# Feed-forward through 32 moment and position features per 128-long segment instead of all 512 inputs, weights built once, and one state chunk in eight weighed on VectorE

## The chip, the cores and the metric

One of the eight cores of a Trainium2 chip runs the whole program in one launch. The metric is the device time of one execution in microseconds (us). TensorE (PE; its weight loads are PEld), VectorE (DVE), ScalarE (ACT), GpSimd (POOL) and SyncE (SP) run side by side and meet only at semaphores.

## What is computed

Two layers over x (4 batches x 512 positions x 512 features). The change lies in the second and third lines:

```
x += attention of layer 0 (keys and queries from ctx), on layernorm(x)
x += down_w @ (silu(gate_w @ h) * (up_w @ h)),   h = layernorm(x)        # 2048 inner rows
x += selective scan (512 channels, 16 states, 512 steps) from ctx, gated by silu(layernorm(x))
x += mixture of experts (32 experts, 8 per token), on layernorm(x)

spline weights:   w[n] = cubic in f between control points,  n = 0 .. 2048*512-1
                  t = linspace(0, NCTRL-1, n);  i = floor(t);  f = t - i      # NCTRL = n / 128.9
scan, per state:  state = state * exp(dt * A) + (dt * u) * B[t];   y += state * C[t]
```

A control point covers 128.9 consecutive weights. So any 128 consecutive weights of a row lie on at most two cubics, that of control interval i and the next, and where the second takes over is known beforehand (the masks).

## The kernel before, in words

Four blocks follow each other: `block_a` (attention, inputs of the scan, and 24 cubic coefficients per 512 weights, `coef_d`), `block_b` (scan and feed-forward), `block_c` (gating, router) and `block_d` (experts). The change is in `block_a` and above all in `block_b`.

`block_b` interleaves two jobs that share no data. The **scan** takes 64 steps `s` (4 batches x 16 states); a step works on four chunks of 128 channels x 512 positions. For each step POOL multiplies the input by the row B (`drive`, L1156) into the tile `E`, ACT makes the decay (`decay`, L889) into one of two banks `dA`, DVE runs the recurrence (`scan`, L1024), POOL multiplies three chunks by the row C (`weigh`, L1162), DVE the fourth, whose state lies in a bank (`weigh_last`, L1030), and a DMA of POOL's queue adds 1 MB of products to `y_d` in HBM (`gather`, L1173). POOL's own order is `weigh(s)`, `drive(s + 2)`, `gather(s)`. `E` has four buffers (`drive(s + 2)` waits until the transfer of step s - 2 has landed), the rows B and C have three between them (`BC`, loaded by SP), `dA` two (`decay` m waits for `scan` m - 2). Each of these chains is in the order written out by hand.

The **feed-forward** takes 32 turns `jj`, two steps each: turn `jj` does 256 inner rows (group `jj // 4`) for one batch (`jj % 4`). The weights of a group are built from coefficients by 6 units (`weights`, `unit_first`, `blend`, `unit_lo`): PE evaluates the two cubics of 128 x 512 weights (L781, L784), DVE picks by mask (L991, L995), ACT and DVE split the result in a high and a low part (L867, L1000). The eight groups take 48 units. A turn's `gate_up` is 2 chunks x 2 matrices x 4 K-slices x 3 products (high*high, high*low, low*high; L794 to L796), 48 matmuls of type fp32r. Then come `silu` (ACT, L879, between two loads of ACT's function table: exp, silu, exp), `mult` (DVE, L1006), `down` (4 tiles x 2 matmuls in full fp32, L806) and four `add`s to x (DVE, L1011). The last `mult` and `down` stand behind the last statistics of x (`late_sums`, L1016).

The two products with the row C before:

```python
            def weigh(s):
                ...
                g.tensor_tensor(E[:, s % NR, 0:NW, :], E[:, s % NR, 0:NW, :], spread(BC[op % NBC][:, :], NW), ALU.mult).then_inc(prod_done, 1)
            def weigh_last(s):
                ...
                v.tensor_tensor(E[:, s % NR, NW, :], dA[(KC * s + NW) % 2][:, :], BC[op % NBC][:, :], ALU.mult).then_inc(last_done, 1)
```

## Time and profile before

| | us |
|---|---|
| median of 3 runs | 1568.68 (1562.31 to 1570.82) |
| span of the profiled execution | 1567.3 |
| up to the end of `block_a` | about 180 |
| `block_b` | about 180 to 818 |
| first `weigh` to the last `weigh` of the 64 steps | 198.66 to 798.60 |
| `block_c` and `block_d` | 818 to 1567.3 |

The profiled execution's time beyond its span is not recorded; its span lies 1.4 us under the median. Busy time over the whole span: PE 1435.0, DVE 1153.4, POOL 1062.3, ACT 918.4. A busy PE is not a PE at its peak, since matmuls overlap in its pipeline; the distance between the starts of two matmuls says more. In the rows below, idle time stands in square brackets with what ended it.

### The profile page before, as it was taken

How to read it: one execution, taken by the hardware profiler on the slowest of the kernel's cores; microseconds unless marked ns; L12 is line 12 of the kernel's file. 1: busy time of each engine (PE TensorE's matmuls, PEld its weight loads, DVE VectorE, ACT ScalarE, POOL GpSimd, SP SyncE). 2: the span in 40 equal slices, each digit the busy share in tenths (PEclk: the TensorE clock that was granted, in tenths of full speed). 3: DMA queues.
4: the chain of work that ended last, by engine and by line, in shares of the span. 5: the costliest groups of instructions: out<-in, count | busy, mean ns of one | idle time of the engine just before them, and what ended most of it. 6: DMA issues, size and time to landing. Idle time of an engine off the chain costs nothing. (4 is left out here: it accounts for less than half of the span.)

```text
span 1567.3 us, 26498 instructions
## 1 busy us (share of the span) xinstructions
PE 1435.0 (92%) x6453; PEld 1073.9 (69%) x6454; DVE 1153.4 (74%) x2069; ACT 918.4 (59%) x1420; POOL 1062.3 (68%) x654
## 2 busy tenths in 40 slices
PE   6999878999999999999975559989999999999997
PEld 3444556666666666666644238878988888898886
DVE  5888897888888878888878786656666666565554
ACT  6777677666667666766646664444544444444442
POOL 2222287999999989999941235757666676666675
PEclk9999989999999999999988759999999999999999
DMA  8232557888899889988869416889998899888876
GB/s 314 96 111 98 180 132 144 179 197 205 192 196 217 186 195 178 221 188 195 176 150 336 159 31 159 193 193 209 198 200 192 191 206 201 203 186 190 189 146 118
DMA packets 106416, 283.95 MB, mean 181 GB/s; under 512 B 16641, under 2 KB 18850, under 8 KB 95090
## 3 DMA queue, kind: packets, MB, share of 16 engines
q0 software_dynamic: 43520, 155.57, 50.0%
q1 hardware_dynamic: 60322, 123.12, 26.4%
q10 hardware_dynamic: 2512, 4.52, 0.8%
q8 instruction: 27, 0.44, 0.1%
q14 instruction: 35, 0.29, 0.1%
HBM read 152.28 MB, written 135.08 MB: 183 GB/s over the span
## 5 line engine op out<-in xcount | busy, mean ns | idle before, releaser
L1156 POOL TENSOR_TENSOR B_E<-B_dtu,B_BC 128x512 f32<-128x512 f32 (+3 forms) x121 | 309.3, 2670 | 16.7 <-DMA B_BC<-bc_d 16.7
L2080 POOL DMA_INDIRECT out_x<-D_y,D_rows x144 | 243.8, 1693 | 75.4 <-issue 43.6
L889 ACT ACTIVATE bank<-B_dtv,negA 128x512 f32<-128x512 f32 x256 | 173.5, 690 | 159.8 <-DVE B_E L1024 98.1
L1024 DVE TENSOR_TENSOR_SCAN B_E<-bank,B_E 128x512 f32<-128x512 f32 x192 | 230.2, 1214 | 42.5 <-ACT bank L889 34.8
L1162 POOL TENSOR_TENSOR B_E<-B_E,B_BC 128x1536 f32<-128x1536 f32 x64 | 234.0, 3656 | 34.5 <-DVE B_E L1024 29.8
L2045 POOL DMA_INDIRECT D_rows<-rows_d,D_source x144 | 155.9, 1083 | 129.0 <-DMA out_x<-D_y,D_rows 62.3
L806 PE MATMUL bank<-B_Wd,B_inter 128*128 128x512 f32 x512 | 231.9, 606 | 9.0 <-DVE X L1011 5.3
L1906 ACT ACTIVATE D_xT_hi<-bank 128x512 fp32r<-128x512 f32 x147 | 88.1, 599 | 231.5 <-PE bank L1815 167.8
L1826 PE MATMUL bank<-W_gu_hi,D_xT_hi 128*128 x584 | 202.4, 347 | 14.5 <-ACT D_xT_hi L1906 13.9
L1968 DVE TENSOR_TENSOR D_xT_lo<-bank,D_xT_hi 128x512 fp32r<-128x512 f32 x147 | 101.3, 689 | 141.1 <-ACT D_xT_hi L1906 108.7
L1827 PE MATMUL bank<-W_gu_lo,D_xT_hi 128*128 x584 | 199.2, 341 | 0.0
L806 PEld LDWEIGHTS bank<-B_Wd,B_inter 128*128 128x128 f32 x512 | 98.3, 195 | 122.8 <-issue 102.8
L1832 PE MATMUL bank<-W_gu_hi,D_xT_lo 128*128 x584 | 131.8, 348 | 6.8 <-DVE D_xT_lo L1968 5.5
L1946 ACT ACTIVATE D_y<-bank 128x512 f32<-128x512 f32 x144 | 86.4, 600 | 83.2 <-PE bank L1899 63.6
L1826 PEld LDWEIGHTS bank<-W_gu_hi,D_xT_hi 128*128 128x128 f32 x584 | 111.1, 190 | 27.5 <-issue 22.2
L1832 PEld LDWEIGHTS bank<-W_gu_hi,D_xT_lo 128*128 128x128 f32 x584 | 103.3, 191 | 18.6 <-DVE D_xT_lo L1968 14.0
L1827 PEld LDWEIGHTS bank<-W_gu_lo,D_xT_hi 128*128 128x128 f32 x584 | 111.2, 190 | 5.5
L794 PE MATMUL bank<-hT_hi,B_Wg_hi 128*128 128x512 f32 x256 | 105.4, 412 | 7.3 <-DVE hT_lo L1064 7.3
L2032 DVE TENSOR_TENSOR W_gu_lo<-W_raw_gu,W_gu_hi x30 | 52.8, 1761 | 66.4 <-ACT W_gu_hi L1916 51.3
L795 PE MATMUL bank<-hT_lo,B_Wg_hi 128*128 128x512 f32 x256 | 100.8, 394 | 0.0
L796 PE MATMUL bank<-hT_hi,B_Wg_lo 128*128 128x512 f32 x256 | 100.3, 392 | 0.0
L1011 DVE TENSOR_TENSOR X<-bank,X 128x512 f32<-128x512 f32 x128 | 86.7, 678 | 18.2 <-PE bank L806 18.2
(327 smaller groups left out, 3263.7 us busy)
## 6 DMA issues: line engine op xcount, KB each, us to landing
y_d<-B_E POOLq DMA_DIRECT2D x64, 1024.0 KB, 10.7
B_BC<-bc_d SPq DMA_DIRECT2D x128, 256.0 KB, 6.2
W_raw_gu<-in_wgu SPq DMA_DIRECT2D x64, 384.0 KB
W_raw_d<-in_wd SPq DMA_DIRECT2D x64, 256.0 KB
X<-in_x SPq DMA_DIRECT2D x4, 1024.0 KB, 9.2
y_d<-A_du SPq DMA_DIRECT2D x4, 1024.0 KB, 4.0
dt_d<-A_dtv SPq DMA_DIRECT2D x4, 1024.0 KB, 3.9
dtu_d<-A_dtu SPq DMA_DIRECT2D x4, 1024.0 KB, 4.1
```

Of the source, the lines that this page charges most:

```text
L794: pe.matmul(ps[:, :], hi, h_hi, start=k == 0, stop=False)
L806: mm = pe.matmul(Yb[t % 2][:, :], chunk(jj, ch)[:, t * P:(t + 1) * P], Wd[w][:, ch, :], start=ch == 0, stop=ch == 1)
L889: act.activation(dA[m % 2][:, :], dtv[:, c, :], ACT.Exp, scale=negA[:, c, n:n + 1]).then_inc(dA_done, 1)
L1024: v.tensor_tensor_scan(state, dA[m % 2][:, :], E[:, s % NR, c, :], 0.0, ALU.mult, ALU.add).then_inc(s_done, 1)
L1156: g.tensor_tensor(E[:, s % NR, c:end, :], dtu[:, at:at + end - c, :], spread(BC[op % NBC][:, :], end - c), ALU.mult).then_inc(dbu_done, 1)
L1162: g.tensor_tensor(E[:, s % NR, 0:NW, :], E[:, s % NR, 0:NW, :], spread(BC[op % NBC][:, :], NW), ALU.mult).then_inc(prod_done, 1)
L1826: pe.matmul(ps, *operands(k, xT_hi, W.gu_hi), start=k == 0, stop=False)
L1827: pe.matmul(ps, *operands(k, xT_hi, W.gu_lo), start=False, stop=False)
L1832: mm = pe.matmul(ps, *operands(k, xT_lo, W.gu_hi), start=False, stop=k == KC - 1)
L1968: v.tensor_tensor(xT_lo[i % 2][:, :], pT[:, :], xT_hi[i % 2][:, :], ALU.subtract).then_inc(xT_sb, 1)
L2045: g.indirect_dma_start(rows[i], None, rows_d[:, :], bass.IndirectOffsetOnAxis(ap=source[i // HALF][:, i % HALF:i % HALF + 1].bitcast(U32), ...
L2080: g.indirect_dma_start(a["out"], bass.IndirectOffsetOnAxis(ap=rows[i][:, ROW - 1:ROW].bitcast(U32), axis=0), ysb[:, i, :], None, compute_o ...
```

## The change

The feed-forward's weights of 128 consecutive inputs are a cubic in the position within the segment, so a product with h needs only the sums of h * position^p (p = 0..3). Instead of multiplying by 512 inputs, each turn first makes 4 x 32 features of h (`features`: for each segment of 128 inputs, the four moments of up to two runs of positions that share one side of every mask, and the few positions left over as they are), and multiplies these 128 features by weights `V` on features. For the runs to be few, the inner rows are sorted by where their second cubic begins, in groups of 256.

Per turn, `gate_up` is then 2 chunks x 2 matrices x 3 products on one K-slice, 12 matmuls; `features` is 4 full-fp32 matmuls with 32 columns of weights each, at four column positions of the array, whose result ACT copies (`feature_hi`) and DVE splits (`feature_lo`). The weights of all groups fit on chip, so they are built once: 24 units in turns 0 to 6 (8 for gate and up with 32 coefficients, 16 for down with 64 rows), in full fp32, with masks and powers loaded four units ahead through ACT's queue. The turns go batch by batch (`jj // 8` is the batch); h is transposed for one batch at a time, at three batch boundaries. `down` sums four chunks of 128 inner rows in one bank (two tiles of x a turn, 4 matmuls each), so there are two `add`s a turn. `silu` runs twice in a row. The last two turns' `down`s come ahead of the last statistics, except for their last two tiles.

In the scan, POOL's `weigh` takes three chunks in even steps and two in odd ones; DVE multiplies the third chunk there, ahead of `weigh_last`. In `block_a` DVE no longer splits the coefficients (12 instructions), the powers are no longer copied by ACT, and the table is loaded in four parts.

```diff
-NSEL = 3 * 2 * KC * 4
+NSEL = 2 * KC * 4
+NCH = INTER // P
+NF = P // KC
+TURN_UNITS = [[("gate_up", 1)] + [("down", k) for k in range(3)]]
+TURN_UNITS += [[("gate_up", g)] + [("down", 3 * (g - 1) + k) for k in range(3)] for g in (2, 3, 4)]
+TURN_UNITS += [[("gate_up", 5)] + [("down", k) for k in range(12, NCH)], [("gate_up", 6)], [("gate_up", 7)]]
+UNITS = [("gate_up", 0)] + [u for units in TURN_UNITS for u in units]
+NAHEAD = 4
...
+            later = second[:, own * KC + c]
+            edges = [0] + [e for e in range(1, P) if (later[e] != later[e - 1]).any()] + [P]
+            runs = sorted(zip(edges[:-1], edges[1:]), key=lambda run: run[0] - run[1])[:2]
+            alone = [e for e in range(P) if not any(lo <= e < hi for lo, hi in runs)]
+            assert 4 * len(runs) + len(alone) <= NF
+            for k, (lo, hi) in enumerate(runs):
+                for p in range(4):
+                    f = 4 * k + p
+                    summed[lo:hi, g, c, f] = power[p, lo:hi]
+                    for ab in range(2):
+                        to[ab, c, p, ab, c * NF + f] = 1.0
+                    masks[g, c * NF + f] = np.tile(later[lo], 2)
+            for k, e in enumerate(alone):
+                f = 4 * len(runs) + k
+                summed[e, g, c, f] = 1.0
+                for ab in range(2):
+                    to[ab, c, :, ab, c * NF + f] = power[:, e]
+                masks[g, c * NF + f] = np.tile(later[e], 2)
...
-                for n in range(3):
-                    v.wait_ge(c_hi, b * 3 + n + 1)
-                    v.tensor_tensor(coef[LOW, n, :], bank[2 + n][LOW, :], coef[LOW, n, :], ALU.subtract).then_inc(c_lo, 1)
...
+        NI, NBC, NR, NDU = 8, 3, 4, KC + 1
+        inter = sb("inter", [P, NI, L])
...
+        def sums_at(jj):
+            return [4 * (jj // 2 - 1) + 2 * (jj % 2) + i for i in range(2)] if jj >= 2 else []
+        def sum_tile(n):
+            return n // 16 * LT + n % 4
+        def pool_chunks(s):
+            return NW - s % 2
...
+            def weights(m):
+                n = unit_job(m)
+                kind, u = UNITS[m]
+                if m >= NAHEAD:
+                    pe.wait_ge(ld_unit[m % NAHEAD], 32 * (m // NAHEAD))
+                if kind == "gate_up" and u:
+                    pe.wait_ge(ld_coef, 16 * (u + 1))
+                if kind == "down" and u == 0:
+                    pe.wait_ge(ld_down, 16 * 2 * NCH // KC)
                 pair_free(n)
...
                 for ab, ps, done in ((0, first_bank(n), a_ps), (1, second_bank(n), b_ps)):
...
+                    if kind == "gate_up":
+                        pe.matmul(ps[:, :], powers[0:NSEL, m % NAHEAD, ab, :], coef[:, :], start=True, stop=True).then_inc(done, 1)
                     else:
-                        mm = pe.matmul(ps[:, :], powers[:, 2 * (g % 2) + unit - 4, ab, :], (coef[:, :] if g else first_down), start=True, stop=True)
-                    mm.then_inc(done, 1)
+                        pe.matmul(ps[:, :], powers[:, m % NAHEAD, 0, :], down_coef[:, ab, :], start=True, stop=True).then_inc(done, 1)
+            def features(jj):
+                g = jj % NG
+                if jj == 0:
+                    pe.wait_ge(ld_coef, 16)
+                if jj:
+                    pe.wait_ge(f_lo, jj)
+                if g == 0:
+                    pe.wait_ge(hT_done, LT * (jj // NG + 1))
+                for c in range(KC):
+                    mm = pe.matmul(F_bank[c * NF:(c + 1) * NF, :], summed[:, g, c, :], hT[:, c, :], start=True, stop=True, tile_position=(0, c * NF))
+                mm.then_inc(f_ps, 1)
             def gate_up(jj, ch):
-                n, w, tb = chunk_job[(jj, ch)], jj // 4 % 2, jj % 4
+                n, g = chunk_job(jj, ch), jj % NG
+                pe.wait_ge(f_lo, jj + 1)
+                if jj < NG:
+                    pe.wait_ge(used, unit_job(unit_of("gate_up", g)) + 1)
                 pair_free(n)
...
+                for ps, col, done in ((first_bank(n), ch * P, a_ps), (second_bank(n), GW + ch * P, b_ps)):
+                    hi, lo = (V[:, g, col:col + P] for V in (V_hi, V_lo))
+                    pe.matmul(ps[:, :], hi, F_hi[:, :], start=True, stop=False)
+                    pe.matmul(ps[:, :], hi, F_lo[:, :], start=False, stop=False)
+                    pe.matmul(ps[:, :], lo, F_hi[:, :], start=False, stop=True).then_inc(done, 1)
+            def down(n, ps):
+                quarter, t = n // 4, n % 4
+                if n < 16:
+                    pe.wait_ge(used, unit_job(unit_of("down", 4 * quarter + 3)) + 1)
+                pe.wait_ge(used, chunk_job(2 * quarter + 1, 1) + 1)
+                if quarter == NB * 4 - 1:
+                    if t >= 2:
+                        pe.wait_ge(add_done, n - 1)
+                elif n:
+                    pe.wait_ge(add_done, n)
+                if t == 0 and quarter == NB * 4 - 1:
+                    pe.wait_ge(add_done, n)
+                for i in range(4):
+                    mm = pe.matmul(ps[:, :], chunk(4 * quarter + i)[:, t * P:(t + 1) * P], Wd[:, (4 * quarter + i) % NCH, :], start=i == 0, stop=i == 3)
+                mm.then_inc(y_ps, 1)
             def turn(t):
                 pe.wait_ge(xn_done, t + 1)
-                if t >= 2:
+                if t % LT >= 2:
                     pe.wait_ge(hT_done, t - 1)
+                elif t >= LT and t % 2 == 0:
+                    pe.wait_ge(f_lo, NG * (t // LT))
+                elif t >= LT:
+                    pe.wait_ge(add_done, sums_at(NG * (t // LT) - 2)[-1] + 1)
                 for k in range(KC):
-                    mm = pe.transpose(Yb[t % 2][:, k * P:(k + 1) * P], xn[t % 2][:, k * P:(k + 1) * P], ident[:, :])
+                    mm = pe.transpose(T_bank[t % 2][:, k * P:(k + 1) * P], xn[t % 2][:, k * P:(k + 1) * P], ident[:, :])
                 mm.then_inc(tr, 1)
-            def two_turns(t):
+            weights(0)
+            for t in range(LT):
                 turn(t)
...
+            features(0)
+            for jj in range(TURNS):
                 gate_up(jj, 0)
...
                 gate_up(jj, 1)
...
+                sums = sums_at(jj)
+                if jj % NG == NG - 1 and jj < TURNS - 1:
+                    for t in range(LT):
+                        turn(LT * (jj // NG + 1) + t)
+                    pe.wait_ge(hT_done, LT * (jj // NG + 2))
+                    down(sums[0], Y_bank)
+                    features(jj + 1)
+                    down(sums[1], Y_bank)
+                else:
+                    if jj < TURNS - 1:
+                        features(jj + 1)
+                    for m in turn_units(jj):
+                        weights(m)
+                    for n in sums:
+                        down(n, Y_bank)
...
+            def load_unit(m):
+                at = m - NAHEAD
+                act.wait_ge(used, unit_job(at) + 1)
+                act.dma_start(powers[:, m % NAHEAD, :, :], a["powers"][m]).then_inc(ld_unit[m % NAHEAD], 16)
+                act.dma_start(words[:, m % NAHEAD, :], a["masks"][m]).then_inc(ld_unit[m % NAHEAD], 16)
...
+            for jj in range(TURNS):
+                tb = jj // NG
                 decay(2 * jj, 2)
                 decay(2 * jj, 3)
                 silu(jj, 0)
-                unit_and_decay(jj, 0, 2 * jj + 1, 0)
-                for c in range(1, KC):
+                silu(jj, 1)
+                if jj == 2:
+                    act.wait_ge(stats, 3)
+                    act.activation(rstd[:, :], rstd[:, :], ACT.Sqrt).then_inc(root, 1)
+                turns = jj % NG == NG - 1 and jj < TURNS - 1
+                units = turn_units(jj)
+                after = [units[0:1], units[1:2], units[2:3], units[3:]] if units else [[]] * KC
+                if turns:
+                    for t in range(2):
+                        turned(LT * (tb + 1) + t)
+                        normal(LT * (tb + 1) + t + 2)
+                elif jj < TURNS - 1:
+                    feature_hi(jj + 1)
...
+            def feature_lo(jj):
+                v.wait_ge(f_hi, jj + 1)
+                v.tensor_tensor(F_lo[:, :], F_bank[:, :], F_hi[:, :], ALU.subtract).then_inc(f_lo, 1)
...
+                for c in range(pool_chunks(s), NW):
+                    v.tensor_tensor(E[:, s % NR, c, :], E[:, s % NR, c, :], BC[op % NBC][:, :], ALU.mult)
...
+            for jj in range(TURNS):
+                tb = jj // NG
                 scan(2 * jj, 2)
                 scan(2 * jj, 3)
+                weigh_last(2 * jj)
+                if jj == 1:
+                    ln_first(REST[LT:]).then_inc(stats, 1)
+                    ln_sums()
+                if jj == 2:
+                    ln_scale()
                 mult(jj, 0)
...
+                mult(jj, 1)
+                turns = jj % NG == NG - 1 and jj < TURNS - 1
+                units = turn_units(jj)
+                sums = sums_at(jj)
+                if jj < TURNS - 1 and not turns:
+                    feature_lo(jj + 1)
+                if units:
+                    blend(units[0])
                 scan(2 * jj + 1, 0)
...
+                if units:
+                    unit_lo(units[0])
+                scan(2 * jj + 1, 1)
+                if sums and not units and not turns:
+                    add(sums[0], Y_bank)
+                for m in units[1:2]:
+                    blend(m)
+                scan(2 * jj + 1, 2)
+                for m in units[2:3]:
+                    blend(m)
+                scan(2 * jj + 1, 3)
+                for m in units[3:]:
+                    blend(m)
                 weigh_last(2 * jj + 1)
-                if jj > NB * NJ - 3:
-                    late_sums(EARLY[(jj + 2 - NB * NJ) * LT:(jj + 3 - NB * NJ) * LT])
+                if sums and (turns or units):
+                    add(sums[0], Y_bank)
+                if jj < TURNS - 1:
+                    scan(2 * jj + 2, 0)
+                    scan(2 * jj + 2, 1)
+                if turns:
+                    feature_lo(jj + 1)
+                if sums:
+                    add(sums[1], Y_bank)
+                if jj > TURNS - 3:
+                    late_sums(EARLY[(jj + 2 - TURNS) * LT:(jj + 3 - TURNS) * LT])
...
             def weigh(s):
                 op = weigh_op(s)
                 g.wait_ge(ld_bc[op % NBC], 16 * (op // NBC + 1))
-                g.wait_ge(s_done, KC * s + NW)
-                g.tensor_tensor(E[:, s % NR, 0:NW, :], E[:, s % NR, 0:NW, :], spread(BC[op % NBC][:, :], NW), ALU.mult).then_inc(prod_done, 1)
+                n = pool_chunks(s)
+                g.wait_ge(s_done, KC * s + n)
+                g.tensor_tensor(E[:, s % NR, 0:n, :], E[:, s % NR, 0:n, :], spread(BC[op % NBC][:, :], n), ALU.mult).then_inc(prod_done, 1)
```

## Rows read from the trace of the kernel before

**Rows 1.** Busy time by stretch; columns: stretch, length, each engine's busy time (x instructions), PEclk, DMA share, GB/s.

```profile
198.70:361.00 162.30, 148.48 (x567) 102.91 (x566) 137.67 (x176) 115.72 (x149) 141.72 (x55) 0.97 0.77 170
361.00:798.60 437.60, 433.88 (x1597) 295.14 (x1596) 367.77 (x432) 292.11 (x360) 420.00 (x196) 1.00 0.89 193
...
270.00:345.00 75.00, 75.00 (x280) 51.40 (x280) 64.03 (x76) 51.28 (x64) 69.94 (x28) 1.00 0.83 178
```

**Rows 2.** Timeline of PE in the scan: start us, us, what.

```profile
518.57 0.40 PE L795 MATMUL bank<-hT_lo,B_Wg_hi 128*128 128x512 f32 x1
518.80 0.39 PE L796 MATMUL bank<-hT_hi,B_Wg_lo 128*128 128x512 f32 x1
...
529.23 0.64 PE L781 MATMUL bank<-coef,powers 96*128 96x256 f32 x4
529.71 7.03 PE L806 MATMUL bank<-B_Wd,B_inter 128*128 128x512 f32 x16
536.18 1.04 PE L781 MATMUL bank<-coef,powers 96*128 96x256 f32 x4
```

**Rows 3.** Timeline of POOL in the scan.

```profile
198.66 3.52 POOL L1162 TENSOR_TENSOR B_E<-B_E,B_BC 128x1536 f32<-128x1536 f32 x1
...
212.02 3.49 POOL L1162 TENSOR_TENSOR B_E<-B_E,B_BC 128x1536 f32<-128x1536 f32 x1 [4.47 <-DVE B_E L1024]
...
360.97 3.47 POOL L1162 TENSOR_TENSOR B_E<-B_E,B_BC 128x1536 f32<-128x1536 f32 x1 [0.26 <-DMA y_d<-B_E]
...
519.16 3.81 POOL L1162 TENSOR_TENSOR B_E<-B_E,B_BC 128x1536 f32<-128x1536 f32 x1
522.62 5.06 POOL L1156 TENSOR_TENSOR B_E<-B_dtu,B_BC 128x1024 f32<-128x1024 f32 x2
527.32 0.86 POOL L1171 DMA_DIRECT2D y_d<-B_E  x1
527.91 3.76 POOL L1162 TENSOR_TENSOR B_E<-B_E,B_BC 128x1536 f32<-128x1536 f32 x1
...
798.60 3.50 POOL L1162 TENSOR_TENSOR B_E<-B_E,B_BC 128x1536 f32<-128x1536 f32 x1 [2.27 <-DVE B_E L1024]
```

**Rows 4.** Waits, 361 to 798.6 us: who, for what, us in total, times, longest.

```profile
POOL B_E L1162 <- DVE B_E L1024: 10.5, 15, 2.3
```

**Rows 5.** Timeline of DVE in the scan: two recurrences in a row.

```profile
521.08 2.33 DVE L1024 TENSOR_TENSOR_SCAN B_E<-bank,B_E 128x512 f32<-128x512 f32 x2
```

**Rows 6.** Groups by line and shape, 190 to 802 us: count, busy, mean ns, idle before.

```profile
L1011 DVE TENSOR_TENSOR X<-bank,X 128x512 f32<-128x512 f32 x124 | 84.0, 677 | 10.9 <-PE bank L806 10.9
L879 ACT ACT_TABLE_LOAD x64 | 82.1, 1283 | 2.0 <-PE bank L806 0.9
```

**Rows 7.** Transfers that read the tile `E`: us to landing.

```profile
DMA to landing us min/median/max: 6.0/10.7/13.9
```

**Rows 8.** Timeline of POOL, then of DVE, in `block_c`.

```profile
837.52 3.41 POOL L1316 TENSOR_TENSOR W_gu_lo<-W_raw_gu,W_gu_hi 128x1536 fp32r<-128x1536 f32 x1
847.10 2.36 POOL L1319 TENSOR_TENSOR W_d_lo<-W_raw_d,W_d_hi 128x1024 fp32r<-128x1024 f32 x1 [6.17 <-DVE X L1394]
...
840.00 3.08 DVE L1441 TENSOR_TENSOR W_d_lo<-W_gu_hi,W_d_lo 128x2048 f32<-128x2048 f32 x1 [2.55 <-DMA W_gu_hi<-y_d]
...
848.67 2.94 DVE L1441 TENSOR_TENSOR W_d_hi<-W_gu_lo,W_d_hi 128x2048 f32<-128x2048 f32 x1
```

**Rows 9.** Groups by line, first 190 us: DVE, POOL idle beside it.

```profile
L515 DVE TENSOR_TENSOR A_dtv<-A_pos,A_ln 128x2048 f32<-128x2048 f32 x4 | 9.2, 2292 | 0.0
```

**Rows 10.** Busy time by stretch around a gap of PE.

```profile
204.00:208.00 4.00, 0.48 (x2) 0.44 (x3) 4.00 (x7) 3.95 (x6) 3.55 (x2) 1.00 0.54 151
208.00:212.00 4.00, 4.00 (x13) 3.11 (x12) 3.93 (x15) 3.94 (x6) 0.00 (x0) 0.57 1.07 139
```

**Rows 11.** Timeline behind the last scan: PE, DVE.

```profile
807.52 9.65 PE L806 MATMUL bank<-B_Wd,B_inter 128*128 128x512 f32 x16 [3.76 <-DVE B_inter L1006]
...
817.20 0.69 DVE L1011 TENSOR_TENSOR X<-bank,X 128x512 f32<-128x512 f32 x1 [1.02 <-PE bank L806]
```

613 lines of the change are left out of this document (236 added, 377 removed).

## The prediction, as put on record before the result

> **What bounds the kernel now.** I read the busy time by stretch first. The change touches the scan and the feed-forward beside it, from the first `weigh` at 198.66 us to the last at 798.60 [rows 3]. Behind the first eight turns PE is busy 433.9 of 437.6 us and POOL 420.0, while DVE has 367.8 and ACT 292.1 [rows 1]. Two engines are full, so I cost each of them per turn (two steps).
>
> PE: the starts of two matmuls of gate and up are 0.23 us apart, a unit takes 0.48, and the 8 matmuls of a `down` take from 529.71 to 536.18, which is 6.47 or 0.81 each [rows 2]. A turn without units is 48 x 0.227 + 6.47 = 17.4 us. POOL: from one `weigh` to the next without a wait it is 519.16 to 527.91, 8.75 us a step, of which the first 3.46 are the `weigh` itself [rows 3]. Two steps are 17.5. So without units both engines need the same 17.4, and with two units PE needs 18.4 and idles a little between them. Measured: 360.97 to 798.60 is 437.6 us for 47 steps, 9.31 a step or 18.6 a turn. POOL's waits for the recurrence are only 10.5 us in there [rows 4]. The transfers are the third full resource: share 0.89 [rows 1], or 0.89 x 9.31 = 8.3 us a step. The first eight turns are worse: 198.66 to 360.97, 162.3 us, 20.3 a turn, with waits like the 4.47 us ahead of 212.02 [rows 3].
>
> **The change part by part.**
>
> *PE.* A steady turn becomes 12 x 0.227 = 2.7 for gate and up, 8 x 0.81 = 6.5 for `down` and 4 full-fp32 feature matmuls. No row has a matmul with 32 columns of weights at its own place in the array. The nearest is `down`'s at 0.81 each, so 3.2 us; if the four ran together it would be 0.8. I take 3.2. The sum is 12.4 us instead of 17.4 to 18.4. PE stops being a bound.
>
> *POOL.* In odd steps the `weigh` has two chunks. Three take 3.46 (522.62 - 519.16) and two 2.36 (`block_c`, 128x1024) [rows 3, 8]. So 1.1 us goes per turn: 17.5 - 1.1 = 16.4. This is the new floor.
>
> *DVE.* Two recurrences in a row take 2.33, about 1.12 for each one that another follows [rows 5], and every other 512-wide instruction 0.68 alone [rows 6], some 0.61 back to back. After: 8 x 1.12 + 8 others (2 `weigh_last`, 1 new product, 2 `mult`, 1 `feature_lo`, 2 `add`) x 0.61 = 13.9 us. Before it was 8 + 8 as well, plus blends and splits (1.5 units a turn): two of the four `add`s go, and the feature split and the new product take their place.
>
> *ACT.* Two silus in a row need two table loads a turn instead of four, 2 x 1.28 = 2.6 us less [rows 6]. The chain silu, silu, features, table, decay still ends about 5.7 us behind the second recurrence of the even step, where DVE arrives after 5.2, so DVE waits some 0.5: 14.4 us. By that sum DVE has 2 us of slack against POOL's 16.4.
>
> *The new product.* This is the step I trust least. It is DVE's only instruction in the scan with both inputs in SBUF (the others read a bank). `block_c` shows two such: 128x2048 products at 840.00 and 848.67 that take 3.08 and 2.94 us, while POOL multiplies SBUF tiles until 840.93 and 849.46 [rows 8]. With POOL idle the same size takes 2.29 [rows 9]. 0.93 and 0.79 us lay before the end of POOL's instruction, and 3.08 - 0.93 = 2.15 and 2.94 - 0.79 = 2.15: DVE stood still until POOL's instruction ended. POOL is busy nearly all the time in the scan, so the product waits for the end of what POOL is in: between 0 and a whole `drive`, 4.7 us (522.62 to 527.32 [rows 3]). While POOL is the bound, DVE runs ahead by most of a step and reaches the product in the middle of a `drive`; the wait comes out of its 2 us of slack. If it is more, DVE falls back and meets the `drive` later, so the wait shortens itself. I take a turn of 16.4 plus 0.3 for what POOL loses when DVE goes first (between 0 and 0.6, the product's own length). Whether POOL in turn is held up, no row shows. The Trainium skill, SBUF — State Buffer, "SBUF: two separate sides", says that a VectorE instruction with two SBUF inputs and a GpSimd instruction that reads SBUF exclude each other for the whole instruction, whichever starts first. By the rule POOL loses up to 0.6 us a turn, by the rows alone nothing.
>
> *Transfers.* Masks and coefficients (640 KB in 8 steps, of some 13 MB) end with turn 6. That leaves about 7.9 of 8.3 us a step, for steps of 8.4. The add into `y_d` must land before `drive(s + 2)`: from its issue there are 0.6 + 8.75 + 3.46 = 12.8 us now and 11.7 then, for 10.7 in the median and 13.9 at most [rows 7]. I add 0.2 us a turn (0 to 1.4). Steady turn: 16.9.
>
> *PE's clock.* PE now waits for `add` between the two `down`s, some 4 us a turn. In the trace a gap of 3.5 us (204 to 208) is followed by a stretch at a mean clock of 0.57 [rows 10], that is, 3.4 of 4 us at 1.2 GHz instead of 2.4: 1.7 us of PE's work. 12.4 + 1.7 = 14.1, still under 16.4. Taken as nothing, at most 0.5 a turn.
>
> *First eight turns.* Four units a turn, each 2 x 0.81 = 1.6 us of PE and one or two DVE instructions: PE 12.4 + 6.5 = 18.9, DVE 13.9 + 5 x 0.61 = 17. DVE is the bound here, so POOL follows it closely and the new product meets a fresh `drive`: 4 us more. Turns 0 to 7: 20, 24 (statistics of 8 tiles), 22, 22, 23, 18, 18, 21 = 168, for 162.3 before. Bounds 155 and 185.
>
> *Batch boundaries.* h is transposed at two boundaries in the rest: four transposes, copies, features in a chain ahead of the next gate and up. 2 us each (0 to 6).
>
> *Ends.* `block_a` loses 12 DVE instructions, but PE is busy 9 tenths of it; 1 us. The tail: `down` now starts at 807.52 behind the statistics and the last `add` stands at 817.20 [rows 11]; half of it will have run, 2.5 us less.
>
> **Sum**: 47 steps at 8.45 = 397 + 4 = 401 against 437.6, -36.6; first turns +5.7; ends -3.5. In all -34: a span of 1533 for 1567.3. The median of the runs lies 1.4 above the profiled span, so I predict **1535 us**.
>
> **The rivals.**
> 1. *Transfers bind.* For it: share 0.89 now and a margin of 1 us to landing. Against it: the stretch of 270 to 345 us, without a boundary, has 0.83 at the same pace [rows 1]. A step of 8.9 instead of 8.45 gives 47 x 0.45 = 21 us back: 1556.
> 2. *Everything hides.* Turns of 16.4 and the first eight in 160: 47 x 8.2 = 385 + 2, -50.6, -2.3, -3.5: 1512.
> 3. *The new product costs a full `drive` in every odd step* (slower). If DVE never gets ahead of POOL, `weigh` begins right behind the second recurrence, `drive` 2.4 us later, and the product, 2.8 us behind that recurrence, waits for 4.2 us more. The turn is 14.4 + 4.2 = 18.6 plus 0.6 for the `gather` that waits for DVE: 19.2. 23.5 x 19.2 = 451 + 4, +18; first turns +10, ends -3.5: 1593. It decides once DVE's own turn, without the wait, is above some 15.5 us instead of 14.4. Against it: POOL needs 16.4 whatever DVE does, and falls behind a DVE that needs less.
> 4. *The change doesn't do what it says*: PE stays at the lower clock, 24.8 us a turn. But then PE has no gap left, and stretches without gaps are all at full clock [rows 1]. I give it nothing of its own; short spells belong to the forecast.
>
> **How the numbers follow.** The forecast has 0.58, with its own range of 1524 to 1547; rival 1 has 0.18, rival 2 0.14, rival 3 0.10. Half a per cent (7.8 us) is about what a measurement of this kernel can tell from no change. Forecast and rival 2 are faster, of rival 1 some two thirds: 0.84. The rest of rival 1 and an edge of rival 3 are the same: 0.07. Slower: 0.09. The range for 8 in 10 goes from 1510 to 1562: it leaves out most of rival 3 and the low edge of rival 2.
>
> **What would show it.** Behind the first eight turns `weigh` to `weigh` over two steps should be about 16.9 us, with PE busy less than 8 tenths, POOL still 9 tenths and more. The DVE product should take from 0.6 to 5 us, with a mean near 2 to 2.5, and end right behind a POOL instruction. `weigh` in odd steps should be 2.4 us. The first eight turns should be no faster than now. I am wrong if POOL has long waits for the recurrence there (rival 3), if it waits for landings of `y_d` or of the rows B and C (rival 1), or if DVE waits for PE.

## The result and the profile after

The changed kernel takes 1688.4 us (median of six runs, 1664.3 to 1697.9) against 1569.0 us for the kernel before (six runs, 1562.3 to 1575.6): ratio 1.070, 95% interval 1.063 to 1.078. The ratio is taken from the three runs in the faster of the kernel's two states (1664.3 to 1686.2), so it is lower than the 1.076 of the two medians. I had forecast 1535 us, in a range that ended at 1562. The profiled execution is the quickest of the six, 1664.3 us with a span of 1662.6; all stretches below are its.

First the busy time by stretch, cut at the first `weigh`, at the first of step 16 and at the last, as the first two of [rows 1] (columns as there):

```profile
198.77:419.07 220.30, 168.83 (x372) 72.56 (x371) 150.86 (x170) 98.23 (x138) 132.16 (x54) 0.72 0.62 136
419.07:888.16 469.09, 319.13 (x872) 147.94 (x870) 432.63 (x379) 235.28 (x321) 392.36 (x195) 0.84 0.81 172
```

The first eight turns went from 162.3 to 220.3 us, the other 47 steps from 437.6 to 469.1. Together that is 89.5 of the 95.3 us between the two spans; 3.5 lie between the last `weigh` and the start of `block_c`, 1.5 in `block_c` and 0.8 in `block_d`, which the change leaves as good as untouched. PE fell from full to 319 of 469 us, as forecast. But POOL did not become the bound: DVE did, with 432.6 of 469.1, 65 us more than before [rows 1], though my sum gave it no more instructions a turn than it had. The groups by line and shape of DVE in the second stretch say which one it is (count, busy, mean ns, idle before):

```profile
L1063 DVE TENSOR_TENSOR_SCAN B_E<-bank,B_E 128x512 f32<-128x512 f32 x140 | 165.2, 1207 | 15.0 <-ACT bank L950 14.9
L1070 DVE TENSOR_TENSOR B_E<-B_E,B_BC 128x512 f32<-128x512 f32 x23 | 117.4, 5105 | 6.0 <-DMA B_BC<-bc_d 3.8
...
L1071 DVE TENSOR_TENSOR B_E<-bank,B_BC 128x512 f32<-128x512 f32 x47 | 32.2, 685 | 8.5 <-DMA B_BC<-bc_d 6.3
L1049 DVE TENSOR_TENSOR X<-bank,X 128x512 f32<-128x512 f32 x47 | 31.2, 665 | 6.3 <-PE bank L861 6.3
```

All of one size, and all near 0.68 us as in [rows 6], except the recurrence and the new product, L1070: 23 of them take 117.4 us, 5.1 each. L1071 beside it has the same shape and reads a bank where L1070 reads `E`. The waits of the stretch show where those microseconds surface: ACT's decays wait for the `weigh_last` behind the product, and PE's `down` for `add`, which is queued behind both on DVE.

```profile
ACT bank L950 <- DVE B_E L1071: 150.3, 25, 12.1
PE bank L861 <- DVE X L1049: 118.8, 34, 9.0
ACT bank L950 <- DVE B_E L1063: 67.4, 107, 2.2
POOL B_E L1179 <- DVE B_E L1063: 41.6, 15, 5.1
```

The last line answers to the 10.5 us of [rows 4]. Now one product in time order, POOL first, then DVE:

```profile
448.24 0.84 POOL L1190 DMA_DIRECT2D y_d<-B_E  x1
448.86 2.60 POOL L1179 TENSOR_TENSOR B_E<-B_E,B_BC 128x1024 f32<-128x1024 f32 x1
451.16 4.97 POOL L1172 TENSOR_TENSOR B_E<-B_dtu,B_BC 128x512 f32<-128x512 f32 x2
457.81 0.87 POOL L1190 DMA_DIRECT2D y_d<-B_E  x1 [1.68 <-issue]
...
448.07 1.21 DVE L1063 TENSOR_TENSOR_SCAN bank<-bank,B_E 128x512 f32<-128x512 f32 x1
449.38 7.30 DVE L1070 TENSOR_TENSOR B_E<-B_E,B_BC 128x512 f32<-128x512 f32 x1
456.61 0.68 DVE L1071 TENSOR_TENSOR B_E<-bank,B_BC 128x512 f32<-128x512 f32 x1
```

The product starts 0.5 us into a two-chunk `weigh`. By the records POOL's instructions leave no room between them: each of the two pieces of the `drive` begins 0.3 us before the one ahead of it has ended. It does not get in where `weigh` ends and `drive` begins (451.2), nor between the two pieces of the `drive`. It ends 0.6 us behind the `drive`, in the time in which POOL stands still for it: the `gather` waits for `last_done`. Of the 32 products 25 end like that, 0.55 or 0.56 us behind the end of a POOL product, with POOL's next one beginning no sooner than they end (to 0.01 us); the other seven, which found POOL idle or came within 0.15 us of the end of its instruction or the start of its next, take 0.68 to 0.79 us. The longest of all, 10.93 us, goes past the end of a `drive`, a DMA issue, a `weigh` and a whole `drive` in four pieces:

```profile
534.16 5.25 POOL L1172 TENSOR_TENSOR B_E<-B_dtu,B_BC 128x512 f32<-128x512 f32 x2
538.75 1.49 POOL L1190 DMA_DIRECT2D y_d<-B_E  x1
539.35 3.32 POOL L1179 TENSOR_TENSOR B_E<-B_E,B_BC 128x1024 f32<-128x1024 f32 x1
541.69 5.83 POOL L1172 TENSOR_TENSOR B_E<-B_dtu,B_BC 128x512 f32<-128x512 f32 x4
549.21 0.87 POOL L1190 DMA_DIRECT2D y_d<-B_E  x1 [1.69 <-issue]
...
537.15 10.93 DVE L1070 TENSOR_TENSOR B_E<-B_E,B_BC 128x512 f32<-128x512 f32 x1
```

In the first eight turns the product is not the cause: six of its eight take 0.68 to 1.35 us, two 5.5 and 4.9 (of all 32, 18 take over 2.6; the expectation of e1 says 20). There the waits are another picture:

```profile
POOL B_E L1179 <- DVE B_E L1063: 63.2, 12, 9.3
...
DVE X L1049 <- PE bank L861: 25.5, 9, 4.5
ACT B_V_hi L922 <- DVE bank L1024: 21.1, 7, 9.0
PE bank L820 <- DVE B_inter L1040: 20.1, 6, 8.8
ACT B_Wd L927 <- PE bank L822: 17.2, 10, 7.0
```

PE waits for DVE, DVE for PE, ACT for both: a chain through the units, with PE at a mean clock of 0.72 between the two levels (1.2 GHz is 0.5, 2.4 GHz is 1). PE's timeline of turn 2 shows what a unit costs in it:

```profile
254.20 1.07 PE L833 MATMUL bank<-B_hT,B_summed 128*32 128x512 f32 x8
264.10 3.75 PE L820 MATMUL bank<-coef,powers 32*128 32x512 f32 x4 [8.83 <-DVE B_inter L1040]
267.78 10.73 PE L822 MATMUL bank<-B_down_coef,powers 64*128 64x512 f32 x12
278.44 6.32 PE L861 MATMUL bank<-B_Wd,B_inter 128*128 128x512 f32 x8
285.64 3.67 PE L861 MATMUL bank<-B_Wd,B_inter 128*128 128x512 f32 x8 [0.88 <-DVE X L1049]
```

PE stood still for 8.83 us, then worked at the lower level (mean clock 0.50 from 264.1 to 278.4): 3.6 us a unit, where I had put 1.6, and 6.3 for the first tile of `down`, 3.7 for the second. And what held DVE until 263.3 is no product of 512 columns at all, but the layer norm's shift for 8 tiles, 128x8 with two SBUF inputs, behind a `drive` on POOL:

```profile
258.85 4.49 POOL L1172 TENSOR_TENSOR B_E<-B_dtu,B_BC 128x2048 f32<-128x2048 f32 x1
...
258.87 0.20 DVE L1088 RECIPROCAL B_rstd<-B_rstd 128x8 f32<-128x8 f32 x1 [1.65 <-ACT B_rstd L981]
259.11 4.25 DVE L1090 SCALAR_TENSOR_TENSOR B_shift<-B_mv,B_rstd 128x8 f32<-128x8 f32 x1
```

### The profile page after: what moved, and what is told of

The parts are those of the page before. It is cut to its first block and busy times, and to the rows that moved or that the text cites. A ratio compares the mean times of both kernels' runs of the same rounds, so it can differ in the third digit from the quotient of the medians.

```text
span 1662.6 us, 24540 instructions
## 1 busy us (share of the span) xinstructions
PE 1344.9 (81%) x5493; PEld 888.1 (53%) x5494; DVE 1221.0 (73%) x1993; ACT 837.7 (50%) x1363; POOL 1017.3 (61%) x656
## 5 line engine op out<-in xcount | busy, mean ns | idle before, releaser
L861 PE MATMUL bank<-B_Wd,B_inter 128*128 128x512 f32 x512 | 305.1, 752 | 153.5 <-DVE X L1049 139.2
L861 PEld LDWEIGHTS bank<-B_Wd,B_inter 128*128 128x128 f32 x512 | 118.2, 242 | 340.6 <-issue 325.3
L2094 POOL DMA_INDIRECT out_x<-D_y,D_rows x144 | 233.3, 1620 | 82.2 <-issue 43.3
L1179 POOL TENSOR_TENSOR B_E<-B_E,B_BC 128x1536 f32<-128x1536 f32 x64 | 196.8, 3075 | 107.7 <-DVE B_E L1063 105.5
L1070 DVE TENSOR_TENSOR B_E<-B_E,B_BC 128x512 f32<-128x512 f32 x32 | 133.4, 4169 | 6.4 <-DMA B_BC<-bc_d 3.8
L1846 PEld LDWEIGHTS bank<-W_gu_hi,D_xT_lo 128*128 128x128 f32 x584 | 103.2, 192 | 21.5 <-DVE D_xT_lo L1982 17.3
L1829 PE MATMUL bank<-ident,D_rows 128*128 128x128 f32 x588 | 90.2, 277 | 5.1 <-DMA D_rows<-rows_d,idx_all 4.4
L596 POOL TENSOR_TENSOR A_dtu<-A_dtv,A_u 128x2048 f32<-128x2048 f32 x4 | 18.1, 4524 | 106.9 <-DVE A_dtv L554 106.9
L1829 PEld LDWEIGHTS bank<-ident,D_rows 128*128 128x128 f32 x588 | 74.6, 143 | 12.4 <-DMA D_rows<-rows_d,idx_all 5.0
```

Of the source, the lines that this page charges most:

```text
L861: mm = pe.matmul(ps[:, :], chunk(4 * quarter + i)[:, t * P:(t + 1) * P], Wd[:, (4 * quarter + i) % NCH, :], start=i == 0, stop=i == 3)
L1070: v.tensor_tensor(E[:, s % NR, c, :], E[:, s % NR, c, :], BC[op % NBC][:, :], ALU.mult)
L1179: g.tensor_tensor(E[:, s % NR, 0:n, :], E[:, s % NR, 0:n, :], spread(BC[op % NBC][:, :], n), ALU.mult).then_inc(prod_done, 1)
L1829: mm = pe.transpose(pT[:, k * P:(k + 1) * P], rows[i][:, k * P:(k + 1) * P], ident[:, :])
L1846: mm = pe.matmul(ps, *operands(k, xT_lo, W.gu_hi), start=False, stop=k == KC - 1)
L2094: g.indirect_dma_start(a["out"], bass.IndirectOffsetOnAxis(ap=rows[i][:, ROW - 1:ROW].bitcast(U32), axis=0), ysb[:, i, :], None, compute_o ...
```

## The experiments

My theory was that two separate things cost the time: in the 47 steps the product is kept out while POOL's instructions follow each other without a hole; in the first eight turns the chain of the units is long, mostly for PE's time at its lower clock. The rivals: PE's clock and the chain of features everywhere; the extra instruction as such; and my prediction's reading, that the product waits for one POOL instruction only. Times are medians; each ratio is to the kernel before on the same chip, whose median there lay between 1565.5 and 1572.4 us for the experiments. The two columns of stretches are cut like those above, each from one profiled execution.

| kernel | us | ratio (95%) | first 8 turns | 47 steps | product, mean us |
|---|---|---|---|---|---|
| before | 1569.0 | 1 | 162.3 | 437.6 | none |
| changed | 1688.4 | 1.070 (1.063 to 1.078) | 220.3 | 469.1 | 4.17 |
| e1 | 1609.7 | 1.024 (1.018 to 1.029) | 210.0 | 425.7 | none |
| e2 | 1593.5 | 1.012 (1.005 to 1.019) | 209.8 | 403.9 | 0.69 |
| e3 | 1709.1 | 1.088 (1.081 to 1.094) | 190.4 | 550.8 | 5.07 |
| e4 | 1585.1 | 1.008 (1.002 to 1.013) | 184.2 | 428.4 | none |
| e5 | 1564.0 | 0.998 (0.995 to 1.002) | 184.6 | 408.9 | 0.7, from the bank |
| e6 | 1580.4 | 1.008 (1.004 to 1.011) | 174.0 | 432.4 | 0.7, from the bank |
| e7 | 1700.7 | 1.085 (1.078 to 1.093) | 221.7 | 507.2 | 5.95 |
| e8 | 1636.6 | 1.044 (1.038 to 1.051) | 212.7 | 447.1 | 3.25 |
| e9 | 1558.1 | 0.994 (0.991 to 0.997) | 168.3 | 413.3 | 0.7, from the bank |
| e10 | 1552.0 | 0.990 (0.987 to 0.994) | 164.2 | 411.7 | 0.7, from the bank |
| e11 | 1580.1 | 1.006 (1.004 to 1.009) | 190.7 | 415.2 | 0.7, from the bank |

**e1, the product handed back.**

```diff
         def pool_chunks(s):
-            return NW - s % 2
+            return NW
```

> The changed kernel with the product handed back: GpSimd weighs chunks 0 to 2 in every step and VectorE only the last. Theory (starved product): in the steady half VectorE's two-input product waits over whole runs of GpSimd instructions (2.6 to 10.9 us in 20 of the 32 steps) and holds its own queue, so without it the 47 steps of 469.0 us fall to about 415 us, near 17.5 us a turn, which is GpSimd's own work; the first eight turns (220.2 us), where the product mostly took 0.68 us, gain at most 10. Median near 1605 us. Rival (TensorE at its lower clock and the chain of features are the cause everywhere, the long products only a symptom): the 47 steps stay within 10 us of 469 and the median at 1665 to 1690. Second rival (no gain because GpSimd's 1.17 us a turn come back on the path): 47 steps at 460 or more.

The 47 steps fell by 43.4 us to 425.7 (I had said about 415), the first turns by 10.3. DVE fell from 432.6 to 321.6 us busy there, 111 us for 23 instructions. The rival of the clock is refuted for this stretch: PE's mean clock is 0.86 against 0.84, and the time went all the same.

**e2, the same product with one SBUF input.**

```diff
-                    v.tensor_tensor(E[:, s % NR, c, :], E[:, s % NR, c, :], BC[op % NBC][:, :], ALU.mult)
+                    v.tensor_tensor(E[:, s % NR, c, :], dA[(KC * s + NW) % 2][:, :], BC[op % NBC][:, :], ALU.mult)
```

> The changed kernel, with the extra product reading a PSUM bank in place of the state chunk in SBUF, so it has one SBUF input instead of two; same length, same place, same order on both engines (the third chunk's own product is left out in every other step). Theory (it is the second SBUF input that keeps it out while GpSimd works): the 32 products take 0.6 to 0.8 us each instead of 4.2, the 47 steps fall to about 400 us (16.4 to 17.0 a turn), median near 1590 us. Rival (one more instruction in VectorE's order does it, or the clock): mean of the product over 2 us or the 47 steps at 455 or more, median as the changed kernel's.

The group of the product, and the two stretches:

```profile
L1070 DVE TENSOR_TENSOR B_E<-bank,B_BC 128x512 f32<-128x512 f32 x32 | 22.0, 689 | 17.1 <-DMA B_BC<-bc_d 14.8
```

```profile
203.94:413.74 209.80, 165.18 (x372) 71.37 (x371) 141.06 (x170) 96.65 (x137) 131.71 (x54) 0.74 0.65 143
413.74:817.60 403.86, 299.34 (x875) 141.19 (x874) 334.54 (x381) 239.91 (x324) 392.02 (x196) 0.87 0.91 198
```

Same place, same length, same output tile; only the first input moved from SBUF to a bank. The kernel leaves out the third chunk's own product in odd steps; e5 makes it properly. No product takes more than 0.69 us, and the 47 steps lose 65 us. POOL is now busy 392.0 of 403.9 us: it is the bound that I had forecast, and 403.9 is 3 us from my 401 (in part by luck, see below). So it was not the instruction but where it reads. The first turns stay at 209.8: their loss is another one.

**e3, the product alone in the old kernel.**

```diff
+                for c in range(NW - s % 2, NW):
+                    v.tensor_tensor(E[:, s % NR, c, :], E[:, s % NR, c, :], BC[op % NBC][:, :], ALU.mult)
...
-                g.wait_ge(s_done, KC * s + NW)
+                n = NW - s % 2
+                g.wait_ge(s_done, KC * s + n)
```

> The kernel before with the product alone: GpSimd weighs three and two chunks by turns, VectorE multiplies the third in odd steps; feed-forward, units and order as before. Theory (starved product): products of 3 to 10 us in the steady half, VectorE falls behind, the 47 steps (437.6 us) grow to 450 to 480, the first eight turns (162.3) by up to 10; median 1.01 to 1.03 of the kernel before. Rival (the product is harmless, the new feed-forward is the cause): GpSimd's 1.17 us a turn come off the time, 47 steps at 410 to 425, median 0.985 of before.

Worse than I expected by far: 1.088, and the 47 steps at 550.8 us, the first turns at 190.4. The busy time of that stretch:

```profile
388.76:939.51 550.75, 468.14 (x1586) 296.97 (x1585) 498.02 (x453) 289.02 (x358) 395.12 (x197) 0.95 0.74 154
```

DVE is busy 498.0 us, POOL only 395.1. With four `add`s and the blends DVE has little slack to lose (367.8 of 437.6 us busy before, [rows 1]), so turn after turn takes the same 23.3 us (17 of the last 23 turns), and POOL's waits for the recurrence are:

```profile
POOL B_E L1165 <- DVE B_E L1024: 109.8, 24, 5.1
```

That is 24 waits of 4.6 us in the mean, where [rows 4] had 10.5 in all. This is the loop of my third rival, at a higher price. The old kernel pays more for the product than the new one: the new feed-forward is not what makes it dear.

**e4, units in one pass** (e1's product, rounded operands; the weights come out less exact).

```diff
-            powers = s.enter_context(nc.sbuf_tensor("powers", [2 * NSEL, NAHEAD, 2, P], F32))
+            powers = s.enter_context(nc.sbuf_tensor("powers", [2 * NSEL, NAHEAD, 2, P], F32R))
...
-        down_coef = sb("down_coef", [2 * NSEL, 2, D])
+        down_coef = sb("down_coef", [2 * NSEL, 2, D], F32R)
```

> The kernel of e1 with TensorE's unit products (the weights on plain and moment columns) in one pass over rounded operands instead of full fp32 (the weights come out less exact; the powers pass through a DRAM copy at the start so that the tiles are of the rounded type). Theory (first eight turns are bound by TensorE's part of the unit chain at its lower clock, 7.0 us for two units): the units fall to about a quarter, first eight turns from about 210 to 175 to 185 us, the steady half as e1, median near 1575 us. Rival (the chain is bound by VectorE's order and its waits, not by TensorE's time): first eight turns within 8 us of e1's.

As expected: the first turns fell from 210.0 to 184.2, the rest stayed. The down units in the first turns, changed kernel (in e1 they take 53.2 us) and then e4 (groups as above):

```profile
L822 PE MATMUL bank<-B_down_coef,powers 64*128 64x512 f32 x64 | 52.3, 985 | 8.4 <-DMA masks<-in_masks 6.1 <-DVE B_V_lo L1034 2.3
```

```profile
L826 PE MATMUL bank<-B_down_coef,powers 64*128 64x512 f32 x32 | 17.5, 640 | 25.4 <-DVE B_V_lo L1038 11.8 <-DMA masks<-in_masks 11.4 <-DVE B_Wd L1032 2.2
```

Between these two 34.8 us of PE's time went there, and 11.7 with the gate and up units; e4's turns are 25.8 us shorter than e1's, so about half of the 46.5 came off the time. The rest was given back as waits: PE now waits for DVE and for the masks.

**e5, the product made properly from the bank, on top of e4.** In odd steps the third chunk's scan leaves its state in the bank of its decay.

```diff
-                state = E[:, s % NR, c, :] if c < NW else dA[m % 2][:, :]
+                state = E[:, s % NR, c, :] if c < NW - s % 2 else dA[m % 2][:, :]
...
+                if s and s % 2 == 0 and c == 0:
+                    act.wait_ge(last_done, last_until(s - 1) - 1)
...
+                for c in range(NW - s % 2, KC):
+                    v.tensor_tensor(E[:, s % NR, c, :], dA[(KC * s + c) % 2][:, :], BC[op % NBC][:, :], ALU.mult).then_inc(last_done, 1)
```

> Two remedies together, with nothing left out: the one-pass units of e4, and in odd steps the third chunk's scan leaves its state in the PSUM bank that held its decay (as the fourth's does), so that VectorE's product reads the bank and one row in SBUF; ScalarE's next decay into that bank waits for the product. Theory: products of 0.7 us, the 47 steps near e2's 403.9 us plus up to 6 for the new wait of the decay, first eight turns as e4's 184.2 or a few less; median 1555 to 1572, 0.99 to 1.00 of the kernel before. Rival (the bank held longer puts ScalarE's decay, then VectorE's scan, on the path): 47 steps above 420 and median above 1575.

The 47 steps take 408.9 us, 5 more than e2 for the new wait of ACT's decay; 15 of the 23 turns take 16.2 to 17.3 us. With the less exact units of e4 the kernel is level with the one before.

**e6, that same form in the old kernel**, and the product in odd steps ahead of the unit's low part.

```diff
+                weigh_last(2 * jj + 1)
                 units(jj, 1, "low")
...
-                weigh_last(2 * jj + 1)
```

> The kernel before with its own feed-forward, and only the product moved in this other form: in odd steps the third chunk's state stays in its PSUM bank and VectorE multiplies from there (its product moved ahead of the unit's low part so that the decay that waits for it can run). Theory (the extra VectorE work is harmless once it reads one SBUF operand): against the 550.8 us of e3 the 47 steps fall to 415 to 430, under the 437.6 of before, since GpSimd loses 1.17 us a turn; median 1550 to 1565, ratio 0.985 to 0.997. Rival (VectorE, busy 84% there, has no room for 0.69 us more, or the transfers bind): 47 steps 435 or more, ratio 1.00 to 1.02.

Half right. The product is harmless (432.4 us, not 550.8), but POOL's 1.17 us a turn bring only 5 us, and the first turns lose 12. The stretch says why:

```profile
373.19:805.55 432.36, 432.09 (x1589) 291.88 (x1588) 380.51 (x453) 287.61 (x359) 394.97 (x197) 1.00 0.91 196
```

PE is busy 432.1 of 432.4 us. It was the second bound of [rows 1], and behind it POOL's time is worth little: the two halves of this change need each other. The new feed-forward alone has 425.7 us (e1), the shorter POOL alone 432.4, both together 408.9 (e5). Why the first turns lose 12 us I did not follow up.

**e7, POOL cut to one chunk an instruction** (the `weigh` as below, and the `drive` likewise).

```diff
-                g.tensor_tensor(E[:, s % NR, 0:n, :], E[:, s % NR, 0:n, :], spread(BC[op % NBC][:, :], n), ALU.mult).then_inc(prod_done, 1)
+                for c in range(n):
+                    i = g.tensor_tensor(E[:, s % NR, c, :], E[:, s % NR, c, :], BC[op % NBC][:, :], ALU.mult)
+                i.then_inc(prod_done, 1)
```

> The changed kernel with GpSimd's instructions cut to one chunk each (about 1.2 us), back to back as before; nothing else. Rival, the prediction's reading (the waiting product gets in at the end of the instruction that GpSimd is in): products of at most about 1.9 us, mean near 1.2, 47 steps near 425. Theory (it isn't served while GpSimd's next instruction is ready, only in a hole of its queue): lengths as before the cut, mean over 3 us and up to 10, 47 steps 455 or more.

This tells the prediction's reading from the theory. POOL, then DVE, around one product:

```profile
609.01 2.76 POOL L1177 TENSOR_TENSOR B_E<-B_E,B_BC 128x512 f32<-128x512 f32 x2
611.47 5.20 POOL L1169 TENSOR_TENSOR B_E<-B_dtu,B_BC 128x512 f32<-128x512 f32 x4
618.37 0.59 POOL L1187 DMA_DIRECT2D y_d<-B_E  x1 [1.69 <-issue]
...
609.62 7.61 DVE L1067 TENSOR_TENSOR B_E<-B_E,B_BC 128x512 f32<-128x512 f32 x1
617.16 0.68 DVE L1068 TENSOR_TENSOR B_E<-bank,B_BC 128x512 f32<-128x512 f32 x1
```

Six POOL instructions of some 1.2 us follow each other, with five ends in between, and the product gets in behind the last (616.67). The mean of all 32 is 5.95 us, the median 7.61. What counts is not how long POOL's instruction is but that the next one stands ready: in the records it begins 0.2 to 0.3 us before the one ahead has ended.

**e8, a hole for it.**

```diff
                 weigh(s)
+                gather(s)
                 if s + 2 < STEPS:
                     drive(s + 2)
-                gather(s)
```

> The changed kernel with GpSimd issuing a step's transfer (which waits for VectorE's last product) right behind its weigh, ahead of the next drive, so that its queue has a hole there. Theory: the product gets in behind the weigh, at most 3.6 + 0.7 = 4.3 us and mean 2 to 3; 47 steps 430 to 455, median 1625 to 1655, though GpSimd stands still meanwhile. Rival (holes don't matter): products up to 10 us as in the changed kernel, 47 steps 469 or more.

The median, 1636.6, and the 47 steps, 447.1, are in the expected range, and the mean of 3.25 us a little over it. But single products reach 7.9 us, where I had set 4.3 as the most. One of them, POOL then DVE:

```profile
669.09 4.96 POOL L1172 TENSOR_TENSOR B_E<-B_dtu,B_BC 128x1024 f32<-128x1024 f32 x2
673.71 2.68 POOL L1179 TENSOR_TENSOR B_E<-B_E,B_BC 128x1024 f32<-128x1024 f32 x1
678.06 0.86 POOL L1190 DMA_DIRECT2D y_d<-B_E  x1 [1.68 <-issue]
...
671.97 4.97 DVE L1070 TENSOR_TENSOR B_E<-B_E,B_BC 128x512 f32<-128x512 f32 x1
```

The product came while the `drive` ran, sat out its rest and the whole `weigh`, and got in where the `gather` waited. I had counted from the start of the `weigh`; the rule held, my starting point did not.

**e9 and e10, the first turns** (on e5, so with its less exact units). e9 moves the layer norm sums (also those ahead of the scan, to turn 8); e10 also deals the down units out more evenly.

```diff
-                if jj == 1:
+                if jj == NG + 1:
                     ln_first(REST[LT:]).then_inc(stats, 1)
                     ln_sums()
-                if jj == 2:
+                if jj == NG + 2:
                     ln_scale()
...
+SPREAD = (0, 2, 4, 6, 8, 11, 14, 16)
+TURN_UNITS = [[("gate_up", g + 1)] + [("down", k) for k in range(SPREAD[g], SPREAD[g + 1])] for g in range(7)]
```

> e5 with the sums of the layer norm of the last two batches (8 bn_stats, 8 bn_aggr, the root and the scale) moved from before the scan and its turns 1 and 2 to turns 8 to 10, where VectorE has room. Theory: the first turns are now bound by VectorE's order between the steps of the unit chain; e5's turns 1 and 2 (26.2 and 32.7 us, where turns 0 and 3 take 19.7 and 21.4) fall to 22 to 26, first eight turns from 184.6 to 170 to 176, the 47 steps stay within 3 us of 408.9; median 1550 to 1558. Rival (those turns are long for their loads of powers and masks or for TensorE at its lower clock): first eight turns within 4 us of 184.6.

> e9 with the 16 down units dealt 2, 2, 2, 2, 3, 3, 2 over turns 0 to 6 in place of 3, 3, 3, 3, 4, 0, 0, each still one turn or more ahead of its first use. Theory: a turn takes two or three units in its gaps and every one beyond lengthens it; first eight turns from about 173 to 160 to 168, steady part unchanged, median 1540 to 1552, 0.984 to 0.992 of the kernel before. Rival (every unit costs the same wherever it stands): first eight turns within 4 us of e9's.

e9: turns 1 and 2 fell from 26.2 and 32.7 to 17.5 and 23.9 us, the first eight to 168.3, below what I expected; 4.4 of the 16.3 us came back in the 47 steps, where the sums now stand, and the median is 1558.1. e10: another 4.1 us in the first turns and 1552.0 us, the quickest of all: 0.990 of the kernel before, and by the two ratios 0.93 of the changed one. The intervals of e9 and e10 overlap, so the runs do not show that the spreading by itself gains anything.

**e11, e10 with full-fp32 units.**

> e10 with its units back in full fp32 and the powers loaded straight from the input, so that against the changed kernel only order and place differ: state of the third chunk in the bank, layer norm sums in turns 8 to 10, down units spread. Theory (two or three full units a turn, at TensorE's lower clock, still make the chain longer than GpSimd's work): first eight turns 178 to 190 against e10's 164.2, the 47 steps within 3 us of 411.7, median 1566 to 1578, no faster than the kernel before. Rival (it was the pile-up of units and sums in turns 0 to 4, not their time on TensorE): first eight turns within 5 us of 164, median about 1555.

The first turns are back at 190.7 us and the median is 1580.1, a little above both ranges. So order and the bank alone are not enough: with the units as exact as in the changed kernel, the best form here is at 1.006 (1.004 to 1.009), still no faster than the kernel before. PE's passes for the units are worth 26.5 us (e11 against e10), the same as the 25.8 from e1 to e4.

## Why the prediction was wrong

The forecast span was 1533, the profiled one 1662.6. Of the 129.6 us, 68 lie in the 47 steps (469.1 for 401), 52 in the first eight turns (220.3 for 168), and 9 outside (+5.8 for -3.5: `block_a` brought nothing, and behind the last `weigh` it is 5.7 longer).

**The failed step is "The new product".** I wrote that the product waits for the end of what POOL is in, 0 to 4.7 us, out of DVE's 2 us of slack, and that a longer wait shortens itself. It waits past ends until POOL's queue has a hole (e7), in 10 of the 23 steady cases 6.7 to 7.6 us and up to 10.9; only in 7 of the 23 does it take under 1.6, so in most turns it does not shorten itself. In the case shown the product starts just behind the start of a two-chunk `weigh`; the rest of it and the `drive` follow without a hole, and only then POOL stops, for this very product. That meeting repeats itself: five of the 23 steady products take 7.29 to 7.31 us. DVE's turn of 13.9 us by my sum becomes 13.9 - 0.6 + 7.3 = 20.6, over POOL's 16.4, and from there DVE paces the loop: eleven of its 23 steady turns take 21.1 to 21.7 us. The chain of cause is shown from both ends: take the second SBUF input away and 65 of the 68 us are gone (e2), put the product into the old kernel and it costs 113 (e3). The Trainium skill, SBUF — State Buffer, "Who interferes with whom", says that a VectorE instruction with at most one SBUF input, outside the modes that use two ports, does not contend with GpSimd, and e2 agrees (0.69 us beside a busy POOL, as alone). It also says that issue order decides who blocks. Here the measurement differs: the product was waiting from 449.4 on, the `drive` began at 451.2 and went first, and in e7 five instructions that began later went first.

The opening says that the engines meet only at semaphores. This product waited for none: beside POOL's work on SBUF it stood still, and it no longer did once its state came from a bank. The other way round it holds as well, which the prediction left open: where a product got in between a `drive` and a `weigh`, the `weigh` began as the product ended (489.33 and 489.34 us, 566.07 and 566.08, 733.78 and 733.78).

The rows that I read it from did not bear it. (They also have the whole `drive` at 5.06 us, not 4.7, which is the way to the DMA issue behind it.) The two products in `block_c` [rows 8] end with POOL's instruction because POOL had nothing ready behind it there: behind the first of the two its next product comes after an idle time of 6.17 us. I saw an instruction's end and a hole of the queue at one instant, and took the first for the cause. The sign that I named, a product that ends right behind a POOL instruction, could not tell the two apart: the long ones do so too. The third rival was this mechanism with one `drive` as its price, and I gave it 0.10: its condition ("once DVE's own turn is above 15.5") was wrong, for DVE need not be behind on its own, the wait puts it there.

**The first eight turns were mis-sized**: +58.0 us where I had put +5.7. My own sums there had PE at 18.9 us a turn and DVE at 17, and yet I called DVE the bound. I priced a unit at 1.6 us of PE at full clock; it took 3.6 at the lower one. I had set PE's clock "as nothing", by a steady turn in which PE has room, and used the same for turns in which it sits in a chain with ACT and DVE. By the runs: the product 10.5 us (e2), the units' passes on PE 25.8 (e4), the layer norm sums in turns 1 and 2 16.3 (e9), the pile-up of down units 4.1 (e10). From 220.3 these lead to about 164 (e10 has 164.2), near the 162.3 of before. Each share is the difference of two profiled executions, taken in that order; another order could divide the sum otherwise.

**What held, and what luck helped.** With the product out of the way POOL is the bound as forecast, and 18 of the 23 turns of e2 take 16.2 to 16.8 us, 16.5 in the mean: the floor of 16.4, without the 0.5 that I had added. That the 47 steps come to 404 us for 401 is in part luck, since turns 10, 18 and 26 take 20.9, 19.8 and 20.9 us, which my sum did not have. There POOL's `drive` waits for the rows B and C (e2, waits of the 47 steps):

```profile
POOL B_E L1172 <- DMA B_BC<-bc_d: 7.1, 3, 2.8
```

That was one of my signs of rival 1, and in these three turns it came true. In the others transfers did not bind (share 0.91 in e2, landing in the median 10.8 us). PE's clock cost nothing in the steady turns: 0.87 in e5, at 16.2 us a turn. The four feature matmuls ran together: 1.07 us for my 3.2, and 0.8 was the other end; it was not on the path. A batch boundary cost 3.4 us instead of 2 (turns 15 and 23 of e2: 19.9 us beside the 16.5). Of the tail, from the last `weigh` to `block_c`, I had expected 2.5 us less; it is 3.5 longer.

**Open**: what happens at a DMA issue between `drive` and `weigh`. This product got in there:

```profile
485.37 3.42 POOL L1172 TENSOR_TENSOR B_E<-B_dtu,B_BC 128x1536 f32<-128x1536 f32 x1
488.74 0.84 POOL L1190 DMA_DIRECT2D y_d<-B_E  x1
489.33 2.62 POOL L1179 TENSOR_TENSOR B_E<-B_E,B_BC 128x1024 f32<-128x1024 f32 x1
...
488.37 0.97 DVE L1070 TENSOR_TENSOR B_E<-B_E,B_BC 128x512 f32<-128x512 f32 x1
```

The longest did not: there the `weigh` began (539.35) before the `drive` had ended (539.41), so there was no hole. The one of 8.91 us at 643.12 did not either, past 0.26 us between the two. Also open is where e6 loses 12 us in its first turns; and whether moving the layer norm sums would help the old kernel too. So not all of e10's gain over it need be this change's, the less as e10's units are less exact.

## What to carry to other kernels

Before work moves to VectorE beside a busy GpSimd, count the SBUF inputs of the instruction. With two, it ran here only when GpSimd's queue had a hole, so its price was the distance to the next hole (up to 10.9 us), not 0.68 us and not one GpSimd instruction. With one operand left in PSUM the price was gone (e2, e5). A wait that is read from a trace has to be read where the other queue is as full as it will be in the new place. And what a unit costs on TensorE has to be priced at the clock of the stretch in which it will stand, above all in a chain where TensorE waits for others.

## What I had not expected of the hardware

- A waiting VectorE instruction is passed by five and more GpSimd instructions that begin after it (e7), and takes up to 10.9 us (changed kernel). A small one waits too: the layer norm's shift of 128x8 took 4.25 us beside a `drive`, and the same operation on 128x4 took 0.16 in `block_c` of the kernel before, with POOL idle.
- Under such a wait the VectorE instruction shows as long, not as late: its record begins right behind the one ahead of it, with no idle time before. What gives it away is the mean by shape (5105 ns), beside a twin that reads a bank (685 ns).
- Four full-fp32 matmuls with 32 columns of weights each, at four places in the array, take 1.07 us together; one of 128 columns takes 0.81 by [rows 2].
